# The first chunks of a feed-forward moved into the norm behind the experts, with that norm's chunk order and pair sums changed

## What is computed

```python
    x = x + _L0_attn_a_ref(_layernorm(x, axis=-1), ...)      # RWKV, then 8 experts, top 2
    x = x + _L0_ffn_ref(_layernorm(x, axis=-1), ...)

    # _L0_ffn_ref: 9 paths of width 32, one chosen per token
    x_mixed = _mix(x, mix_kernel)          # k0*x[t-1] + k1*x[t] + k2*x[t+1]
    h = einsum('bsd,pdm->bspm', x_mixed, W1) + b1
    stacked_paths = einsum('bspm,pmd->bspd', h, W2) + b2
    scores = tanh(x_mixed @ Wo1 + bo1) @ Wo2 + bo2
    idx = argmax(scores, axis=-1)
    collapsed = einsum('bspd,bsp->bsd', stacked_paths, one_hot(idx, P))
    return _layernorm(x + collapsed, gamma, beta)
```

## Time and profile before

| | us |
|---|---|
| median of 3 runs | 1137.93 (1135.59 to 1144.2) |
| profiled execution | 1128.02 |
| its span, first to last instruction | 1126.2 |
| TensorE busy | 1003.1 (89%) |
| VectorE busy | 845.2 (75%) |
| ScalarE busy | 748.8 (66%) |
| POOL busy | 355.0 (32%) |

### The profile page before, as it was taken

How to read it: one execution, slowest core, us unless ns; L and a number is a source line. 1 busy time by engine, 2 the same in 40 slices (tenths; PEclk the granted TensorE clock), 3 DMA queues, 4 the chain that set the end, 5 groups by cost and what they waited for, 6 DMA issues and landing times.

```text
span 1126.2 us, 20922 instructions
## 1 busy us (share of the span) xinstructions
PE 1003.1 (89%) x7682; PEld 622.6 (55%) x7682; DVE 845.2 (75%) x1518; ACT 748.8 (66%) x1235; POOL 355.0 (32%) x457
## 2 busy tenths in 40 slices
PE   7888899688867999899998999889898888898987
PEld 3333544387754444677653444676676775553355
DVE  4998887666654777777755776899999994768866
ACT  6895566345455447456777458687988776768885
POOL 1100057445553112000000114688878773000000
PEclk9999999899998999899999999799999998999999
DMA  7900055466641000000000000000000000000002
GB/s 189 294 0 1 1 150 160 145 200 212 220 145 66 1 0 11 2 2 2 1 2 1 0 1 10 1 3 2 3 2 3 16 3 10 1 1 1 0 1 76
DMA packets 42814, 54.53 MB, mean 48 GB/s; under 512 B 6251, under 2 KB 29372, under 8 KB 42716
## 3 DMA queue, kind: packets, MB, share of 16 engines
q1 hardware_dynamic: 38096, 42.75, 12.9%
q0 software_dynamic: 4288, 10.46, 2.5%
q10 hardware_dynamic: 332, 0.01, 0.0%
HBM read 22.11 MB, written 20.93 MB: 38 GB/s over the span
## 4 chain that ended last, share of the span: by engine, by line
PE 49%; DVE 22%; ACT 15%; issue 9%; POOL 2%; DMA 2%; SPq 0%; ACTq 0%; DVEq 0%
PE psum L88 4%; PE psum L1305 4%; PE psum L1277 3%; PE psum L954 3%; DVE arena L2510 3%; PE psum L1981 3%; DVE N L2519 3%; PE psum L1719 2%; DVE arena L2509 2%; PE psum L905 2%; PE psum L106 2%; ACT ln_std L115 2%; ACT ln_std L117 2%; PE psum L2326 2%; PE psum L918 2%
## 5 line engine op out<-in xcount | busy, mean ns | idle before, releaser
L2336 PE MATMUL psum<-ident,N 128*128 128x128 f32 x512 | 73.2, 288 | 18.4 <-POOL N L2479 17.8
L2425 ACT ACTIVATE N<-N 128x1024 f32<-128x1024 f32 x64 | 67.7, 1059 | 31.7 <-DVE N L2519 30.8
L2326 PEld LDWEIGHTS psum<-arena 32*128 32x128 f32 x1024 | 64.9, 194 | 25.7 <-issue 11.6
L88 PE MATMUL psum<-X,center 128*128 128x512 f32 x128 | 69.4, 631 | 10.6 <-DVE X L1062 4.2
L2326 PE MATMUL psum<-arena 32*128 32x128 f32 x1024 | 77.2, 293 | 1.6 <-ACT arena L2403 1.4
L768 POOL DMA_INDIRECT out_rows<-mixed,out_index x62 | 60.3, 972 | 57.1 <-DVE arena L844 32.0
L95 ACT ACTIVATE ln_sq<-psum 128x512 f32<-128x512 f32 x72 | 42.5, 591 | 52.2 <-PE psum L88 52.1
L2421 ACT ACTIVATE arena<-psum 128x1024 f32<-128x1024 f32 x64 | 65.7, 1026 | 16.9 <-PE psum L2336 16.7
L106 PE MATMUL psum<-ln_sq,mean 128*128 128x512 f32 x144 | 74.3, 607 | 2.1 <-ACT arena L151 1.1
L2336 PEld LDWEIGHTS psum<-ident,N 128*128 128x128 f32 x512 | 57.6, 146 | 28.1 <-POOL N L2479 22.9
L2479 POOL TENSOR_TENSOR N<-N,arena 128x512 f32<-128x512 f32 x64 | 67.8, 1059 | 0.0
(11 more groups left out here) (399 smaller groups left out, 2694.9 us busy)
## 6 DMA issues: line engine op xcount, KB each, us to landing
arena<-weights SPq DMA_DIRECT2D x31, 320.0 KB, 2.6
slot_rows<-zeros SPq DMA_DIRECT2D x1, 8060.0 KB, 26.6
arena<-slot_rows SPq DMA_DIRECT2D x31, 260.0 KB, 3.2
arena<-tw_rows SPq DMA_DIRECT2D x16, 256.0 KB, 3.6
arena<-out_rows SPq DMA_DIRECT2D x6, 512.0 KB, 5.0
out_dram<-arena SPq DMA_DIRECT2D x8, 256.0 KB, 2.8
arena<-in_L_attn_a_x_dram SPq DMA_DIRECT2D x3, 512.0 KB, 6.7
weights<-in_L_attn_a_eWk_dram SPq DMA_DIRECT2D x1, 1024.0 KB, 5.8
```

The lines of the kernel that those rows point to most:

```text
L88: self.nc.tensor.matmul(k.bank[c % W][:], k.center[:], self.src(c), start=True, stop=True).then_inc(k.ln_centered, 1)
L2326: op = nc.tensor.matmul(scored[half][:, e * P:(e + 1) * P], k.sg_Q[b % 2][at, seg, 2 * j:2 * j + 2, :].rearrange("p h n -> p (h n)"), k.sg ...
L2336: op = nc.tensor.transpose(turned_to[:, e * P:(e + 1) * P], pr[n % 4][:, e * P:(e + 1) * P], k.ident[:])
L2425: nc.scalar.activation(pr[n % 4], pr[n % 4], ACT.Exp).then_inc(k.sg_exp, 1)
```

## The change

It does five things.

1. VectorE's list in `combined`: both scales of chunks 0 and 1 come first, then `begin` for both. In call 0 `begin` now mixes chunk c at c = 0 and 1, and folds W2 at c = 1. The mixes at c = 2 and 4 remain for call 1 only.
2. `total` moves from POOL to VectorE: the pair sums of chunks 2 and 3 stand behind `begin`, and the sum of chunk c + 2 stands right behind the residual add of chunk c.
3. TensorE's list in `combined`: the W1 products of chunk 0 (`first_hidden`) stand ahead of the first transposes, those of chunk 1 between the first and the second. The centring of chunk 2 then waits until all six products are copied. Transposes run two chunks ahead.
4. ScalarE copies those products with their bias into `hid` at the start of `combined` (`keep_hidden`). Behind the norm it takes only the two Tanhs, from `hid`.
5. The two memsets that pad W1 move on POOL from behind the experts to `route_constants`, at the kernel's start.

```diff
@@ route_constants, POOL
+        for g in (0, 2):
+            nc.gpsimd.memset(k.W1[:, g, 3 * DM:P], 0.0).then_inc(k.ff_const, 1)
@@ combined
-            nc.gpsimd.tensor_tensor(pair[0], *pair, ALU.add).then_inc(k.cb_sum, 1)
+            nc.vector.tensor_tensor(pair[0], *pair, ALU.add).then_inc(k.cb_sum, 1)
...
+            pe.wait_ge(k.sx_sig, TILES)
+            feed[0](pe, 0)
             turn(pe, DENSE)
-            for c in range(DENSE, NCH + 2):
-                if c + 1 < NCH:
-                    turn(pe, c + 1)
+            feed[0](pe, 1)
+            turn(pe, DENSE + 1)
+            feed[0](pe, DENSE)
+            for c in range(DENSE, NCH + 1):
                 if c < NCH:
                     norm.center(pe, c)
+                if DENSE + 2 <= c + 2 < NCH:
+                    turn(pe, c + 2)
                 if DENSE <= c - 1 < NCH:
                     norm.variance(pe, c - 1)
...
+            for c in range(DENSE):
+                feed[2](act, c)
             norm.square(act, DENSE)
...
             for c in range(DENSE):
                 norm.scale(dve, c)
+            for c in range(DENSE):
                 feed[1](dve, c)
+            total(dve, DENSE)
+            total(dve, DENSE + 1)
             for c in range(DENSE, NCH + 2):
                 if c < NCH:
                     add(dve, c)
+                if c + 2 < NCH:
+                    total(dve, c + 2)
                 if c >= DENSE + 2:
                     norm.scale(dve, c - 2)
                     feed[1](dve, c - 2)
@@ feedforward
+    def first_hidden(pe, c):
+        if c < 2:
+            pe.wait_ge(k.ff_w_in, 16 * (NP + 7))
+            pe.wait_ge(k.ff_const, 2)
+            pe.wait_ge(k.ff_mix, c + 1)
+            for j in range(GR):
+                pe.wait_ge(k.ff_hid, c * 3 + (j + 1))
+                nc.tensor.matmul(k.bank[j][:], k.W1[:, j, :], xm[c], start=True, stop=True).then_inc(k.ff_h, 1)
+        else:
+            pe.wait_ge(k.ff_hid, 6 + PRIMED["ff_hid"])
+
+    def keep_hidden(act, c):
+        for j in range(GR):
+            act.wait_ge(k.ff_h, c * 3 + (j + 1 + PRIMED["ff_h"]))
+            nc.scalar.activation(hid[c][:, j * CH:(j + 1) * CH], k.bank[j][:], ACT.Identity, bias=k.vec(f"b1_{j}")).then_inc(k.ff_hid, 1)
...
+        if c < 2 and call == 0:
+            dve.wait_ge(k.ln_out, k.ln_done - NCH + 2)
+            mix(dve, 0, c)
...
-        if c in (2, 4):
+        if c in (2, 4) and call == 1:
...
-        if c == NCH - 1 and call == 0:
+        if c == 1 and call == 0:
...
+                            act.wait_ge(k.ff_hid, 3 * c0 + 1 + PRIMED["ff_hid"])
+                            nc.scalar.activation(u[c0][2 * DM:3 * DM, :], hid[c0][2 * DM:3 * DM, 0:CH], ACT.Tanh).then_inc(k.ff_u, 1)
```

More of the change, by code:

```diff
@@ L1052, in turn, with total @@
             op.then_inc(k.cb_turned, 1)
-        def total(pool, c):
-            pool.wait_ge(k.sx_rows[c % 4], 16 * (len(range(c % 4, TILES, 4)) + (c - DENSE) // 4 + 1))
+        def total(dve, c):
+            dve.wait_ge(k.sx_rows[c % 4], 16 * (len(range(c % 4, TILES, 4)) + (c - DENSE) // 4 + 1))
             pair = [returned[:, c % 4, :, j, :] for j in range(2)]
-            nc.gpsimd.tensor_tensor(pair[0], *pair, ALU.add).then_inc(k.cb_sum, 1)
+            nc.vector.tensor_tensor(pair[0], *pair, ALU.add).then_inc(k.cb_sum, 1)
         def add(dve, c):
@@ L1081, in _ @@
                 norm.deviation(act, c)
-        @block.gpsimd
-        def _(pool):
-            for c in range(DENSE, NCH):
-                total(pool, c)
         @block.vector
@@ L1181, in begin @@
                 nc.vector.tensor_scalar(k.W2[0:rows, j, :], k.W2[0:rows, j, :], k.W2_sum[0:rows, j:j + 1], None, ALU.add).then_inc(k.ff_fold, 1)
-    normalize((lambda pe, c: None, begin))
+    normalize((first_hidden, begin, keep_hidden) if call == 0 else (lambda pe, c: None, begin))
     normed = k.ln_done
@@ L1189, in _ @@
         if call == 0:
-            for g in (0, 2):
-                nc.gpsimd.memset(k.W1[:, g, 3 * DM:P], 0.0).then_inc(k.ff_const, 1)
             for p in range(NP):
@@ L1315, in turn @@
                 if first and c == 0:
-                    hidden(it, 0, True)
+                    if call == 1:
+                        hidden(it, 0, True)
                     pe.wait_ge(k.ln_out, normed)
@@ L1323, in turn @@
                 scores(it, c)
-                if first and c == 0:
+                if first and c == 0 and call == 1:
                     hidden(it, 1)
@@ L1362, in turn @@
                 if first and c == 0:
-                    hidden(it, 0)
-                    hidden(it, 1)
+                    for c0 in range(2):
+                        if call == 1:
+                            hidden(it, c0)
+                        else:
+                            act.wait_ge(k.ff_hid, 3 * c0 + 1 + PRIMED["ff_hid"])
+                            nc.scalar.activation(u[c0][2 * DM:3 * DM, :], hid[c0][2 * DM:3 * DM, 0:CH], ACT.Tanh).then_inc(k.ff_u, 1)
                 else:
```

## The result

The changed kernel takes 1146.28 us (median of 20 runs, 1141.47 to 1151.66), the kernel before 1138.28 us (median of 20, 1131.03 to 1154.0). The ratio is 1.0067, 95% interval [1.0047, 1.0087]: slower by 0.7%, some 7.6 us. Some executions fall into a slower state, and the ratios and means of this text leave those out. The measured median is inside the range that was predicted (1131 to 1147), 0.7 us from its upper end, the change is inside the 1% that the prediction called no change, and in its direction, but three times its size (+2.3 us).

A forecast was written before the change was run, and what follows sets the result against it. Bound: the chain of waits up to the first spread, then TensorE, and TensorE's clock. 5.4 + 1.7 - 5.85 - 1.65 + 2.7 = +2.3 us on 1128.02, so 1130.3; with the runs' 9.9 step, 1140 (range 1131 to 1147).

The forecast's parts named there:

- First term: Ahead of chunk 2's centring: longer VectorE list makes it 5.4 us later, plus 1.7 for two slow products.
- C: Start of chunk 2's centring product on TensorE: 340.40 us before, predicted at 347.5, bounds 345.8 and 349.
- Second term: Norm's loop, chunk 2's centring to the scores: 24.15 us before, 18.3 predicted, a gain of 5.85.
- Third term: Scores to first spread: 5.21 us before, 3.55 without chunk 1's products and copies between, a gain of 1.65.
- Fourth term: Behind the norm: emptied TensorE falls to half clock, costing 1.0 us before the spread and 1.7 behind, +2.7 together.
- the stretch: The part the change touches; measured from VectorE's scale of chunk 0 to the table load at the feed-forward's end.
- (a): Rival: the clock holds behind the norm, leaving the dependency sum alone, -2.1 us, 1136; chance 0.25.
- (b): Rival: TensorE stays at half clock through the feed-forward's first turns, up to 17 us; +9, 1147; chance 0.1.
- (c): Rival: late centring of chunk 2 eats the gain, no clock fall behind; within 0.5 us of zero, 1138; chance 0.1.

The follow-up runs named there:

- `fold_last`: The changed kernel with only the folding of W2 moved back behind the last scale; median 1142.53 us, ratio 1.0023 to the kernel before.
- `sums_only`: The kernel before with pair sums on VectorE and sums and transposes two chunks ahead, nothing of the feed-forward moved; ratio 0.9996 to the kernel before.
- `fill_after`: The changed kernel plus five unread TensorE products, four behind the last variance, one behind the scores; median 1135.18 us, ratio 0.9976 to the kernel before.
- `fill_after2`: The changed kernel plus nine unread TensorE products: four behind the variances of chunks 0 and 1, four behind the norm, one behind the scores; ratio 1.0007 to before.
- `after_again`: The changed kernel, unchanged, run again for a second ratio and profile; median 1145.69 us, ratio 1.0043 to the kernel before.

## Why the prediction was right, and where it was off

**First term, right.** The first sum was predicted 10.3 us behind the scale of chunk 0 (341.2 - 330.87) and came at 10.6. C was predicted at 347.5, which is 16.6, between 14.9 and 18.1; it came at 17.0, 15.3 and 15.5 in three executions. The half clock at chunk 1's products, taken as certain in the sum and priced at 1.7 us, occurred in the first of these only, and cost 1.7 there (the three products 4.00 for 2.74, the transposes ahead of them 1.11 for 0.66). At full clock C was due at 14.9 and came 0.4 to 0.5 later. (The base, 340.40, is the chain's figure; the timeline starts that product at 340.19, 9.3 behind the scale, and against that C moved by 7.7, 6.0 and 6.1 for the 7.1 forecast.) The fold alone is worth 1.85 of it (`fold_last`).

**Second term, the size right, a reason wrong.** 18.3 us were predicted from C to the scores, and 18.4 measured in every kernel without a mix in the loop. The text gave two causes, the mixes and the order two chunks ahead. `sums_only` shows that the order alone gives nothing; the mixes alone were not tried.

**Third term, right as a dependency sum.** 3.55 us predicted, 3.55 measured where the clock held (`fill_after`). In the changed kernel it took 5.2, 4.1 and 4.8 us, since the clock was down; the text had named 3.5 to 4.6 as the sign of being right, and two of the three lie outside.

**Fourth term, the mechanism right, the size too small.** The fall came where predicted. It was priced at 2.7 us (1.0 between scores and spread, 1.7 behind). Against the full-clock times 3.56 and 45.59 the three executions paid 5.4, 3.8 and 5.2 (1.6 + 3.8, 0.6 + 3.2, 1.2 + 3.9). The mis-sized part is mainly the work bound by TensorE at half clock: 3.4 us were assumed, while the clock stayed down until 387.1 with the spread at 378.8, some 8 us. The clock did come back with TensorE at work, at 387.1 us. The Trainium skill (TensorE: Matmul & The Clock Gate, Part 1, "What's actually happening") says that activity releases the throttle; the trace agrees in kind. Why it came back only then, 8 us behind the spread, no run here settles.

**The sum.** Predicted +2.3 us. The stretch took 89.95, 86.65 and 88.12 us with the change (mean 88.2), and 84.48, 84.68 and 87.80 without (mean 85.7): +2.6. That the two figures agree is partly luck, as errors cancel: the clock's price was 2 us larger, but C came half a microsecond earlier on the mean, and the kernel before paid such falls too, 3.2 us in one of three executions, which the prediction had excluded. Against the one profile that the prediction started from, the changed kernel's mean is +3.8.

**Outside the stretch.** The measured difference, 7.6 us (interval 5.3 to 9.9) in the first comparison and 4.9 in the second (0.8 to 8.9), is more than 2.6, and the prediction had nothing for the rest. It said that the rest of the program stands in the same order, and took it that what the first spread gains or loses is all that changes. Behind the stretch the three profiles took 714.7, 719.9 and 710.0 us, before 710.8, 710.2 and 710.5, in stages with unchanged lists. Their time at half clock there was 52.5, 58.7 and 34.5 us, before 38.3, 34.9 and 42.3, so where they took more, the clock was down longer. Over all executions the changed kernel has 8 to 15 us more at half clock, while the stretch shows 3.4 more on the mean of the three profiles of each. That speaks for further falls elsewhere in the run as the rest of the loss. Where they lie in executions without a trace, and how the change would bring them about in stages that it leaves alone, no run here shows. `fill_after` has the same lists behind the stretch and took 708.8 there.

**The rivals.** (a), the clock holds, did not happen in the changed kernel; `fill_after` shows what it would have been worth in the stretch: 1.6 us against the profile that the prediction started from (82.9 for 84.5), where the text had 2.1, and 2.8 against the mean of before (85.7). (b), half clock through the first turns, came true in part: 13.6 us, not 17, and only 8 of them bound. Its median, 1147, is nearer to the 1146.28 measured than the forecast's 1140, but by another way than it gave: in the stretch its +9 did not happen. (c) did not happen.

## What to carry to other kernels

An instruction moved out of a wait is free only if the wait that it leaves has other cover and the place that it moves to has none to lose: here a fold of 1.85 us went from beside a table load to the path, and six products left the place where, in two of the three profiles of the kernel before, the clock stayed up. When a change empties an engine's list, read the granted clock there and price the bound work behind the hole at half speed; unread products are a quick test of that price, but a fall held off in one place may come in a dearer one (`fill_after2`, in one execution). And take a second profile of the kernel before: clock falls that one execution does not show cost it 3 us in another.

## What the runs showed of the hardware

A busy TensorE did not always get its clock back soon. In `after_again` it was busy 13.20 of 13.20 us at 0.50 in the FAVOR stage, and had been at half clock for 20.5 us in all, with the same instructions that got the full clock after 6.8 us in the kernel before.

One 128x512 pair sum in f32 takes 0.64 us on VectorE and 1.27 on POOL (two in 1.28 and 2.54). On two chips the same kernel reached the scale of chunk 0 at 329.83 and 337.55 us, and its medians were 1128.78 and 1137.87.
